# Holding V in the array and streaming the attention weights, in a fused scan, attention and expert kernel

## The chip, the cores and the metric

One Trainium2 chip, one of its cores. The metric is the device time of one execution in microseconds (us); of several executions the median is given. The engines are TensorE (PE in the rows, its weight loads PEld), VectorE (DVE), ScalarE (ACT) and GpSimd (POOL); SP is the queue that issues the transfers.

## The reference

The input is 16 sequences of 256 rows of 128 features, f32. Each is normalised over its features, giving xn. The output is x + scan(xn) + ffn(xn). The scan is a depthwise convolution, a step size from a matmul and a sigmoid, and a state recurrence in 16 states. The other branch is what the change touches:

```
h = layernorm(xn, ln_g, ln_b)
q, k, v = h @ Wq, h @ Wk, h @ Wv            # 16 heads of 64
q, k = l2norm(q) * q_scale, l2norm(k) * k_scale
logits = (q @ k^T) * 10, causal mask
attn = softmax(logits)
out = (attn @ v) joined over heads @ Wo
```

Then come another layernorm, a gate (softmax over 8 experts), all 8 experts (128 to 512, gelu, 512 to 128), their gated sum and a last layernorm.

## The kernel before, in words

The sequences run through a software pipeline. `bodies` calls a prologue, 16 times `body(i, ...)` and a tail, on every engine; each engine runs its own list of work in the order in which it is written, and 60-odd semaphores tie them. Body i does the attention of sequence i, the projections of sequence i+1 (`project`, `project_v`), and the output projection and the experts of sequence i-1. A body has two parts.

The **weighing part** is the loop over k from 0 to 9. The 16 heads are worked as 8 pairs. On TensorE (lines 535 to 556) step k issues, in this order: `scores(i, k)` (L398), which fills S2 with logits of pair k, keys in the partitions; `weigh(i, k-1)` (L415); `project(i+1, k)` (L309 to L311), in the last two steps two `project_v`; for k below 2 half of `output(i-1)` (L431); single turns; and `turn_o(i, k-2)` (L422). ScalarE takes the exponential of the scores (`exps`, L674) into P32, a ring of three buffers; GpSimd sets the triangle above the diagonal to zero (`select`, L830) and squares the projections (`square`, L814). So P32 holds, for each head of a pair, the weights P transposed: keys in the partitions, queries along the columns, 256 columns for the first block of 128 keys and 128 columns for the second, since the other queries come before those keys.

`weigh` works in f32. P is held in the array (128 keys by 128 queries) and V is streamed: Vx has 66 columns per head, 64 of values, and a column of ones at 64, whose product is the softmax's sum. For a pair there are six matmuls (two heads, and three blocks of the causal triangle) into four blocks of 66 columns of O[p % 2], with queries in the partitions. An f32 matmul stands in the trace as two MATMUL records with a weight load each, so 12 for a pair. A `transpose` stands as one. `divide` on VectorE (L1018, L1021) takes the reciprocals of the four sums, 4 numbers in a partition, and multiplies them into the 256 values, giving On. `turn_o` transposes On through the array, two transposes, back into O. `copy_ot` on ScalarE (L680) copies that to OT, 64 features by 2 heads in the partitions, queries along the columns, which `output` of the next body holds as weights. O0 and O1 are two banks of PSUM in turns: `weigh(p)` waits for `ot_done` of pair p-2 (line 409).

VectorE's list of the weighing part (lines 1230 to 1256) begins step k with `divide(i, k-2)`, and then `qk_sums(i+1, k-2)` (L967), the steps of three layernorms (`E_AT`, `O_AT`, `G_AT`), and for seven values of k one state of the scan (`SCAN_AT`; L1113 and L1123).

The **expert part** is the loop over m from 0 to 9: the experts of sequence i-1 (L483 to L485, L701, L499, L1084), the turning of q and k of sequence i+1 (L344), and its score maxima (L358, L362, L1012). The remaining nine states of the scan run there on VectorE. GpSimd scales q and k (`units`, L822) around the border of the parts.

Of the kernel before, what the change touches and what calls it, by code (L numbers as in the profile page):

```python
# [10 lines left out]
ACT = mybir.ActivationFunctionType  # L11
AX = mybir.AxisListType

NSEQ, SEQ, D = 16, 256, 128
P = 128
T = SEQ // P
H, DH = 16, 64
NP = H // 2
HD = H * DH
# [2 lines left out]
DS = 16  # L22
NJ = 4 * T
NL = NP
VW = DH + 2
WS = 64.0
LN_EPS, L2_EPS = 1e-5, 1e-12
QK_SCALE = 10.0
# [12 lines left out]
def build(nc, x, a_log, b, c, dt_w, dt_b, conv_w, conv_b, ln_g, ln_b, Wq, Wk, Wv, q_scale, k_scale,  # L41
          Wo, gate_w, gate_b, w1, b1, w2, b2, out):
    ctx = ExitStack()
    with ctx:
        def sb(name, shape, dt=F32):
            return ctx.enter_context(nc.sbuf_tensor(name, shape, dt))

        def sem(name):
# [3 lines left out]
        ident = sb("ident", [P, P])  # L52
# [62 lines left out]
        QTl = sb("QTl", [P, NP, SEQ], F16)  # L115
        KTh = sb("KTh", [P, NP, SEQ], F16)
        KTl = sb("KTl", [P, NP, SEQ], F16)
        Vx = sb("Vx", [P, T, H, VW])

        mxn = sb("mxn", [P, T, 2, P])  # L120
        mT = sb("mT", [P, 2, SEQ], BF16)
        P32 = sb("P32", [P, 3, 2, 2 * SEQ])
        rr = sb("rr", [P, 2, 2 * T])
        On = sb("On", [P, 2, T, 2 * DH])
        OT = sb("OT", [P, NP, SEQ])

        ost = sb("ost", [P, T, 6])
# [53 lines left out]
        O = [ctx.enter_context(nc.psum_tensor(f"O{n}", [P, 512], F32)) for n in range(2)]  # L181
# [5 lines left out]
            g_vec g_act g_tr  # L187
            qk_ready qk_raw qk_sq qk_sum n_vec n_act unit t_ready t_hi t_lo v_ready v_done
            m_ready mx_done mt_ready mt_done
            st_ready ex_done sel_done pv_done rr_done on_done ot_ready ot_done  # L190
            wo_ready wo_copied o_vec o_act o_tr o_gate o_gT o_b2
            w1_ready gelu_done w2_ready acc_done
            c_vec dt_ready tanh_done a_done scan_done y_done
# [4 lines left out]
         g_vec, g_act, g_tr,  # L198
         qk_ready, qk_raw, qk_sq, qk_sum, n_vec, n_act, unit, t_ready, t_hi, t_lo, v_ready, v_done,
         m_ready, mx_done, mt_ready, mt_done,  # L200
         st_ready, ex_done, sel_done, pv_done, rr_done, on_done, ot_ready, ot_done,
         wo_ready, wo_copied, o_vec, o_act, o_tr, o_gate, o_gT, o_b2,
         w1_ready, gelu_done, w2_ready, acc_done,
         c_vec, dt_ready, tanh_done, a_done, scan_done, y_done,
# [12 lines left out]
        def from_one(eng, semaphore, value):  # L217

            if not isinstance(value, int) or value > 0:
                eng.wait_ge(semaphore, value)  # L220
# [72 lines left out]
        def _(pe):  # L293
# [107 lines left out]

            def weigh(s, p, before):

                pe.wait_ge(sel_done, s * NP + p + 1)
                if p == 0:
                    pe.wait_ge(v_done, (s + 1) * 2 * T)
                if p < 2 and before:
                    pe.wait_ge(acc_done, (s - 1) * NE * T - 2 * (1 - p))
                from_one(pe, ot_done, s * NP + p - 1)
                for t in range(T):  # L410
                    for a in range(2):
                        dst = O[p % 2][:, (2 * t + a) * VW:(2 * t + a + 1) * VW]
                        for kb in range(t + 1):
                            c0 = kb * SEQ + (t - kb) * P
                            last = mm(dst, P32[:, p % 3, a, c0:c0 + P], Vx[:, kb, 2 * p + a, :],  # L415
                                      start=(kb == 0), stop=(kb == t))
                last.then_inc(pv_done, 1)

            def turn_o(s, p):
                pe.wait_ge(on_done, s * NP + p + 1)  # L420
                for t in range(T):
                    last = tr(O[p % 2][:, t * P:(t + 1) * P], On[:, p % 2, t, :], ident[:, :])  # L422
                last.then_inc(ot_ready, 1)

            def output(s, t, before):
                if t == 0:
# [107 lines left out]
            def body(i, older, old, new, newer):  # L534
                for k in range(NP + 2):
                    if k < NP:
                        scores(i, k)
                    if k == 0:
                        turn_max(i, 1)
                    if 1 <= k <= NP:  # L540
                        weigh(i, k - 1, older)
                    if new and k < NP:
                        project(i + 1, k)
                    if new and k >= NP:
                        project_v(i + 1, 2 * (k - NP))
                        project_v(i + 1, 2 * (k - NP) + 1)
                    if old and k < T:
                        output(i - 1, k, older)
                    if old and k == 3:
                        turn_y(i - 1)  # L550
                    if old and k == 6:
                        turn_z2(i - 1)
                    if old and k == 7:
                        gate_logits(i - 1)
                    if k >= 2:
                        turn_o(i, k - 2)
                for m in range(NE + 2):
                    if old and m == 0:
                        expert_up(i - 1, 0)
                    if new and m in TURN_AT:  # L560
                        turn_qk(i + 1, TURN_AT[m])
                        turn_qk(i + 1, TURN_AT[m] + 1)
                    if old and m == 1:
                        turn_gate(i - 1, (i + 1) * NP)
                    if new:
                        for p in MAX_AT.get(m, ()):
                            scores_for_max(i + 1, p)
                    if old and 1 <= m < NE:
                        expert_up(i - 1, m)
                    if old and m == 1:  # L570
                        gated_b2(i - 1)
                    if old and 1 <= m <= NE:
                        expert_down(i - 1, m - 1, (i + 1) * NP)
                    if newer and m == 6:
                        turn(i + 2)
                    if new and m == 7:
                        step_sizes(i + 1)
                    if new and m == 8:
                        turn_max(i + 1, 0)
                    if not old and m == NE + 1:  # L580
                        pe.wait_ge(w1_low, 2)
# [20 lines left out]
        def _(act):  # L602
# [27 lines left out]
            def copy_v(s, j):  # L630
                t, w = divmod(j, 2)
                act.wait_ge(v_ready, s * 2 * T + j + 1)
                if j == 0:
                    from_one(act, pv_done, s * NP)
                fn(Vx[:, t, w * 8:(w + 1) * 8, 0:DH], J[j % 2][:, :].rearrange("p (h d) -> p h d", d=DH),  # L635
                   ACT.Copy, scale=1.0 / WS).then_inc(v_done, 1)

            def high(s, n):
# [32 lines left out]
            def exps(s, p):  # L671
                act.wait_ge(st_ready, s * NP + p + 1)
                from_one(act, pv_done, s * NP + p - 2)
                fn(P32[:, p % 3, :, 0:SEQ + P], S2[:, :, 0:SEQ + P], ACT.Exp).then_inc(ex_done, 1)  # L674

            def copy_ot(s, p):
                act.wait_ge(ot_ready, s * NP + p + 1)
                if p == 0:
                    from_one(act, wo_ready, s)
                fn(OT[:, p, :], O[p % 2][:, 0:SEQ], ACT.Copy).then_inc(ot_done, 1)  # L680

            def decay(s, d):

# [59 lines left out]

            def body(i, older, old, new, newer):
                for k in range(NP + 2):
                    if k >= 3:
                        copy_ot(i, k - 3)
                    if old and k == 2:
                        copy_output(i - 1)
                    if k < NP:  # L750
                        exps(i, k)
                    if k == 0:
                        copy_max(i, 1)
                    if new and 1 <= k <= NP:
                        copy_raw(i + 1, k - 1)
                    if older and k == 0:
                        last_norm(i - 2)
                    if old and k == 4:
                        root_o(i - 1)
                    if newer and k == 5:  # L760
                        norm(i + 2)
                    if new and k == 6:
                        norm_qk(i + 1, 0)
                    if k < NP:
                        decay(i, 2 * k)
                        decay(i, 2 * k + 1)
                    if new and k == 9:
                        copy_v(i + 1, 0)
                        copy_v(i + 1, 1)
                    if old and k == 9:  # L770
                        gate_exps(i - 1)
                if new:
                    copy_v(i + 1, 2)
                copy_ot(i, NP - 1)
                if new:
                    copy_v(i + 1, 3)
                    norm_qk(i + 1, 1)
# [109 lines left out]
        def _(dve):  # L887
# [126 lines left out]

            def divide(s, p):
                dve.wait_ge(pv_done, s * NP + p + 1)
                heads = O[p % 2][:, 0:2 * T * VW].rearrange("p (h d) -> p h d", d=VW)
                V.reciprocal(rr[:, p % 2, :].unsqueeze(2), heads[:, :, DH:DH + 1]).then_inc(rr_done, 1)  # L1018
                dve.wait_ge(rr_done, s * NP + p + 1)
                from_one(dve, ot_ready, s * NP + p - 1)  # L1020
                V.tensor_tensor(On[:, p % 2, :, :].rearrange("p t (a d) -> p (t a) d", d=DH), heads[:, :, 0:DH],  # L1021
                                rr[:, p % 2, :].unsqueeze(2).broadcast_to([P, 2 * T, DH]), ALU.mult
                                ).then_inc(on_done, 1)

            def o_step(s, n):
                at = s * KO
# [129 lines left out]
            def prologue():  # L1156
# [3 lines left out]
                V.memset(xnT[:, :], 0.0)  # L1160
                V.memset(gate[:, :, :].rearrange("p t e -> p (t e)"), 0.0)
                V.memset(mxn[:, :, :, :].rearrange("p t g c -> p (t g c)"), 0.0)
                V.memset(Vx[:, :, :, :].rearrange("p t h d -> p (t h d)"), 1.0)
                dve.wait_ge(const_pool, 7)
                V.tensor_copy(identb[:, :], ident[:, :]).then_inc(const_vec, 1)
                V.tensor_copy(maskb[:, :], mask[:, :]).then_inc(const_vec, 1)
# [165 lines left out]
```

## Time and profile before

| | us |
|---|---|
| median of 3 runs | 1340.16 (1338.81 to 1340.35) |
| the profiled execution | 1340.11 |
| its span, first to last instruction | 1338.4 |
| TensorE busy | 1180.9 (88%) |
| VectorE busy | 1048.9 (78%) |
| ScalarE busy | 752.7 (56%) |
| GpSimd busy | 368.5 (28%) |
| mean granted TensorE clock | 0.915 of full speed |

How to read it: the records of matmuls overlap, and their ends are modelled, so what a matmul costs in a row of them is the distance from one start to the next and not its mean duration. 1.7 us of the profiled execution's own time lie outside its span. The chain is followed back from the last instruction to what released each step.

### The profile page before, as it was taken

The numbers are of one execution on the slowest core, as the hardware profiler recorded it, in microseconds if no ns is written. First come the engines' busy times: TensorE is split into PE (matmuls) and PEld (weight loads), VectorE is DVE, ScalarE is ACT, GpSimd is POOL, SyncE is SP. The second block draws the span as 40 slices with busy tenths as digits, with TensorE's granted clock in tenths as the row PEclk, the third lists the DMA queues.
The fourth block names the chain that finished last, engine by engine and source line by source line (L and its number), as shares of the span: only waits on it lengthen the run. The fifth ranks groups of instructions, "written<-read, shape, count | busy, mean of one in ns | idle before, by whom it ended". The sixth has DMA issues, their size and how long they took to land.

```text
span 1338.4 us, 27838 instructions
## 1 busy us (share of the span) xinstructions
PE 1180.9 (88%) x10435; PEld 954.6 (71%) x10435; DVE 1048.9 (78%) x2718; ACT 752.7 (56%) x1740; POOL 368.5 (28%) x403
## 2 busy tenths in 40 slices
PE   3584989899998989989898998989899898989978
PEld 1363768586786868778685877868587786868877
DVE  7779677888878888887888888788888778787652
ACT  4263655556565565656556465655646565564644
POOL 1151422405133150513315051331505133150100
PEclk9595989899998989989898998989999998999889
DMA  6001000000000000000000000000000000000000
GB/s 177 5 1 40 2 1 13 1 9 5 9 5 2 13 1 10 5 9 6 1 13 1 10 5 9 6 1 10 5 9 6 8 7 5 2 9 2 5 5 5
DMA packets 18724, 14.62 MB, mean 11 GB/s; under 512 B 2408, under 2 KB 16160, under 8 KB 18592
## 3 DMA queue, kind: packets, MB, share of 16 engines
q1 hardware_dynamic: 17680, 12.76, 3.3%
q8 instruction: 84, 1.38, 0.4%
q14 instruction: 48, 0.39, 0.1%
q10 hardware_dynamic: 912, 0.09, 0.0%
HBM read 10.75 MB, written 2.10 MB: 10 GB/s over the span
## 4 chain that ended last, share of the span: by engine, by line
PE 76%; DVE 10%; ACT 9%; issue 3%; POOL 0%; SPq 0%; DMA 0%; DVEq 0%; POOLq 0%; ACTq 0%
PE O L499 17%; PE O L415 11%; PE S L398 7%; PE U L431 4%; PE U L483 4%; PE U L484 4%; PE U L485 4%; PE J L344 4%; PE S L362 3%; PE J L309 3%; PE J L311 3%; PE J L310 3%; PE S L358 3%; PE O L422 2%; ACT hid L701 2%
## 5 line engine op out<-in xcount | busy, mean ns | idle before, releaser
L701 ACT ACTIVATE hid<-U,b1c 128x256 f32<-128x256 f32 x512 | 202.9, 474 | 202.1 <-PE U L485 201.2
L830 POOL TENSOR_SCALAR_AFFINE_SELECT P<-P 128x512 f32<-128x512 f32 x128 | 83.8, 655 | 774.3 <-ACT P L674 774.3
L499 PE MATMUL O<-w2s,hid 128*128 128x128 f32 x2048 | 251.5, 276 | 0.0
L499 PEld LDWEIGHTS O<-w2s,hid 128*128 128x128 f32 x2048 | 238.5, 192 | 2.9
L415 PE MATMUL O<-Vx,P 128*128 128x66 f32 x1536 | 200.8, 281 | 9.1 <-ACT OT L680 9.0
L1113 DVE TENSOR_TENSOR_SCAN st<-aexp,u 128x256 f32<-128x256 f32 x256 | 196.9, 769 | 4.7 <-ACT aexp L686 4.7
L415 PEld LDWEIGHTS O<-Vx,P 128*128 128x128 f32 x1536 | 183.0, 193 | 24.1 <-issue 12.5
L822 POOL TENSOR_TENSOR raw<-raw,nr 128x512 f32<-128x512 f32 x128 | 140.2, 1119 | 115.9 <-DVE nr L986 88.8
L483 PE MATMUL U<-h2h,w1h 128*128 128x256 f16 x512 | 149.3, 292 | 0.0
L484 PE MATMUL U<-h2l,w1h 128*128 128x256 f16 x512 | 148.8, 291 | 0.0
L485 PE MATMUL U<-h2h,w1l 128*128 128x256 f16 x512 | 148.0, 289 | 0.0
L1084 DVE SCALAR_TENSOR_TENSOR acc<-O,gate,acc 128x128 f32<-128x128 f32 x256 | 78.0, 346 | 87.2 <-PE O L499 85.3
L344 PE MATMUL J<-ident,raw 128*128 128x128 f32 x512 | 80.3, 305 | 66.5 <-DVE QTl L997 58.9
L674 ACT ACTIVATE P<-S 128x768 f32<-128x768 f32 x128 | 103.8, 811 | 56.8 <-PE S L398 56.6
L1123 DVE SCALAR_TENSOR_TENSOR y<-st,bc,y 128x256 f32<-128x256 f32 x240 | 129.5, 540 | 8.0
L1012 DVE TENSOR_REDUCE mxn<-S 128x2 f32<-128x256 f32 (+1 forms) x256 | 130.1, 551 | 5.9 <-PE S L362 5.6
L814 POOL TENSOR_TENSOR sq<-raw 128x512 f32<-128x512 f32 x120 | 130.5, 1087 | 0.0
L344 PEld LDWEIGHTS J<-ident,raw 128*128 128x128 f32 x512 | 66.1, 158 | 72.7 <-POOL raw L822 67.1
L686 ACT ACTIVATE aexp<-dt,negA 128x256 f32<-128x256 f32 x256 | 115.0, 500 | 0.0
L967 DVE TENSOR_REDUCE ssq<-sq 128x8 f32<-128x512 f32 x128 | 87.2, 681 | 28.9 <-POOL sq L814 28.6
L680 ACT ACTIVATE OT<-O 128x256 f32<-128x256 f32 x128 | 48.8, 381 | 105.8 <-PE O L422 105.7
L309 PE MATMUL J<-wh,hTh 128*128 128x512 f16 x192 | 82.4, 429 | 15.2 <-ACT Vx L635 14.5
(163 smaller groups left out, 2148.6 us busy)
## 6 DMA issues: line engine op xcount, KB each, us to landing
xin<-in_L_attn_x SPq DMA_DIRECT2D x16, 128.0 KB, 2.2
xres<-in_L_attn_x SPq DMA_DIRECT2D x16, 128.0 KB, 2.4
hid<-in_L_ffn_w SPq DMA_DIRECT2D x2, 1024.0 KB, 6.2
out_dram<-fin SPq DMA_DIRECT2D x16, 128.0 KB, 1.8
raw<-in_L_ffn_Wq SPq DMA_DIRECT2D x1, 512.0 KB, 4.3
raw<-in_L_ffn_Wk SPq DMA_DIRECT2D x1, 512.0 KB, 6.6
raw<-in_L_ffn_Wv SPq DMA_DIRECT2D x1, 512.0 KB, 7.5
wos<-in_L_ffn_Wo SPq DMA_DIRECT2D x1, 512.0 KB, 11.0
```

Source lines behind the costliest of these rows:

```text
L344: last = tr(J[n % 2][:, (a * T + t) * P:(a * T + t + 1) * P], raw[:, chunk(t, kind, half), c0:c0 + P], ident[:, :])
L415: last = mm(dst, P32[:, p % 3, a, c0:c0 + P], Vx[:, kb, 2 * p + a, :], start=(kb == 0), stop=(kb == t))
L483: mm(dst, w1h[:, f:f + P], h2h[:, :], start=True, stop=False)
L484: mm(dst, w1h[:, f:f + P], h2l[:, :], start=False, stop=False)
L485: last = mm(dst, w1l[:, f:f + P], h2h[:, :], start=False, stop=True)
L499: last = mm(O[e % 2][:, t * P:(t + 1) * P], hid[:, e % 2, m, t * P:(t + 1) * P], w2s[:, e * FC + m, :], start=(m == 0), stop=(m == FC - 1))
L701: fn(hid[:, e % 2, f % FC, :], U[q % 2][:, m * SEQ:(m + 1) * SEQ], ACT.Gelu_apprx_tanh, bias=b1c[:, f:f + 1], scale=1.0 / WS).then_inc(gel ...
L814: nc.gpsimd.tensor_tensor(sq[:, j % 2, :], raw[:, j, :], raw[:, j, :], ALU.mult).then_inc(qk_sq, 1)
L822: nc.gpsimd.tensor_tensor(group, group, nr[:, j * 8:(j + 1) * 8].unsqueeze(2).broadcast_to([P, 8, DH]), ALU.mult).then_inc(unit, 1)
L1012: V.tensor_reduce(mxn[:, t, g, hh:hh + DH + 2:DH + 1], S2[:, :, t * P:(2 * t + 1) * P], AX.X, ALU.max, negate=True).then_inc(mx_done, 1)
L1113: V.tensor_tensor_scan(st[:, d % 2, :], aexp[:, d, :], u[:, :], 0.0, ALU.mult, ALU.add).then_inc(scan_done, 1)
L1123: V.scalar_tensor_tensor(y[:, s % 2, :], st[:, d % 2, :], bc[:, d:d + 1], y[:, s % 2, :], ALU.mult, ALU.add).then_inc(y_done, 1)
```

## The change

- `weigh` holds V in the array instead of P. A head's V block is 128 keys by 64 values, so it fills half of the array's columns; head 0 of the pair takes columns and output partitions 0 to 63, head 1 takes 64 to 127. P is streamed, 256 columns for the first block of keys and 128 for the second. Columns 0 to 255 of O then hold the weighed values already as features by queries.
- The same four matmuls run a second time with a held 128 by 64 matrix of ones. Columns 256 to 511 of O hold each head's sum, repeated in its 64 partitions.
- `divide` takes the reciprocal of all those 256 columns, and one multiply writes OT.
- `turn_o`, `copy_ot`, On and the ones in Vx are gone. Vx is dense. `ones` is a new tile.

```diff
-        Vx = sb("Vx", [P, T, H, VW])
+        Vx = sb("Vx", [P, T, HD])
+        ones = sb("ones", [P, DH])
-        rr = sb("rr", [P, 2, 2 * T])
-        On = sb("On", [P, 2, T, 2 * DH])
+        rr = sb("rr", [P, 2, SEQ])
...
                 from_one(pe, ot_done, s * NP + p - 1)
-                for t in range(T):
-                    for a in range(2):
-                        dst = O[p % 2][:, (2 * t + a) * VW:(2 * t + a + 1) * VW]
-                        for kb in range(t + 1):
-                            c0 = kb * SEQ + (t - kb) * P
-                            last = mm(dst, P32[:, p % 3, a, c0:c0 + P], Vx[:, kb, 2 * p + a, :],
-                                      start=(kb == 0), stop=(kb == t))
+                for n in range(2):
+                    for kb in range(T):
+                        for a in range(2):
+                            c0 = n * SEQ
+                            values = Vx[:, kb, (2 * p + a) * DH:(2 * p + a + 1) * DH]
+                            last = mm(O[p % 2][a * DH:(a + 1) * DH, c0 + kb * P:c0 + SEQ],
+                                      (values, ones[:, :])[n],
+                                      P32[:, p % 3, a, kb * SEQ:kb * SEQ + SEQ - kb * P],
+                                      start=(kb == 0), stop=(kb == T - 1), skip_group_check=True)
                 last.then_inc(pv_done, 1)
...
             def divide(s, p):
                 dve.wait_ge(pv_done, s * NP + p + 1)
-                heads = O[p % 2][:, 0:2 * T * VW].rearrange("p (h d) -> p h d", d=VW)
-                V.reciprocal(rr[:, p % 2, :].unsqueeze(2), heads[:, :, DH:DH + 1]).then_inc(rr_done, 1)
+                V.reciprocal(rr[:, p % 2, :], O[p % 2][:, SEQ:2 * SEQ]).then_inc(rr_done, 1)
                 dve.wait_ge(rr_done, s * NP + p + 1)
-                from_one(dve, ot_ready, s * NP + p - 1)
-                V.tensor_tensor(On[:, p % 2, :, :].rearrange("p t (a d) -> p (t a) d", d=DH), heads[:, :, 0:DH],
-                                rr[:, p % 2, :].unsqueeze(2).broadcast_to([P, 2 * T, DH]), ALU.mult
-                                ).then_inc(on_done, 1)
+                if p == 0:
+                    from_one(dve, wo_ready, s)
+                V.tensor_tensor(OT[:, p, :], O[p % 2][:, 0:SEQ], rr[:, p % 2, :], ALU.mult).then_inc(ot_done, 1)
```

Besides, `turn_o` and its call are taken from TensorE's list, `copy_ot` and its two calls from ScalarE's, and `copy_v` writes 512 dense columns. Nothing else moves.

## Rows read from the trace of the kernel before

**Rows 1.** The page's chain that ended last, shares of the span.

```profile
PE 76%; DVE 10%; ACT 9%; issue 3%; POOL 0%; SPq 0%; DMA 0%; DVEq 0%; POOLq 0%; ACTq 0%
```

**Rows 2.** Busy time by stretch in one middle body: weighing part (two rows), expert part.

```profile
core 0: us, PE busy (x) PEld busy (x) DVE busy (x) ACT busy (x) POOL busy (x), PEclk, DMA share, GB/s
530.40:552.40 22.00, 21.85 (x235) 18.17 (x236) 15.47 (x54) 16.47 (x38) 9.01 (x11) 1.00 0.03 7
552.40:568.20 15.80, 13.89 (x98) 9.58 (x99) 14.81 (x35) 9.43 (x25) 9.15 (x9) 0.89 0.01 2
568.20:609.10 40.90, 36.48 (x322) 31.48 (x321) 34.07 (x83) 20.29 (x49) 5.29 (x5) 0.92 0.03 8
```

**Rows 3.** Timeline of TensorE, step 3 of that body: start us, us.

```profile
541.92 0.28 PE L398 MATMUL S<-mT,sel 64*128 64x256 bf16 x2
...
542.68 1.55 PE L415 MATMUL O<-Vx,P 128*128 128x66 f32 x12
544.07 0.38 PE L309 MATMUL J<-wh,hTh 128*128 128x512 f16 x1
544.29 0.38 PE L310 MATMUL J<-wh,hTl 128*128 128x512 f16 x1
```

**Rows 4.** Timeline of VectorE, the first `divide` of that body.

```profile
536.48 0.18 DVE L1018 RECIPROCAL rr<-O 128x4 f32<-128x4 f32 x1 [1.64 <-PE O L415]
```

**Rows 5.** The same timeline, the last `divide` of that body.

```profile
565.74 0.18 DVE L1018 RECIPROCAL rr<-O 128x4 f32<-128x4 f32 x1
```

**Rows 6.** VectorE's waits in the weighing part (530 to 571): total us, times, longest.

```profile
DVE rr L1018 <- PE O L415: 3.1, 4, 1.6
DVE ssq L967 <- POOL sq L814: 1.9, 4, 0.6
...
DVE nu L979 <- ACT ny L615: 0.4, 1, 0.4
```

**Rows 7.** Groups by line: count, busy us, mean ns, idle before and releaser.

```profile
L1018 DVE RECIPROCAL rr<-O 128x4 f32<-128x4 f32 x128 | 22.9, 179 | 55.9 <-PE O L415 55.9
L1063 DVE RECIPROCAL grs<-gs 128x2 f32<-128x2 f32 x16 | 2.5, 159 | 0.6 <-ACT ge L669 0.6
L1183 DVE COPY wcol<-J 128x8 f32<-128x8 f32 x1 | 0.2, 157 | 0.0
L1184 DVE COPY b1c<-J 128x32 f32<-128x32 f32 x1 | 0.2, 181 | 0.0
L1074 DVE COPY acc<-O 128x256 f32<-128x256 f32 x16 | 6.8, 425 | 15.1 <-PE O L468 15.1
L1021 DVE TENSOR_TENSOR On<-O,rr 128x256 f32<-128x256 f32 x128 | 54.3, 425 | 4.4
```

**Rows 8.** The two reciprocal lines: ns min/median/max.

```profile
L1018 DVE RECIPROCAL rr<-O x128: 168/182/183, 71.3 to 1261.5; 128x4 f32<-128x4 f32 x128
L1063 DVE RECIPROCAL grs<-gs x16: 157/158/166, 173.4 to 1302.3; 128x2 f32<-128x2 f32 x16
```

**Rows 9.** The chain in order of time: start us, us, what.

```profile
541.77 0.22 PE O L422 x2
...
558.77 0.28 PE O L422 x2
...
559.08 0.39 ACT OT L680
559.47 0.14 issue
```

**Rows 10.** The same view: an f32 matmul of 256 columns, and a projection matmul at the lower clock.

```profile
526.89 0.43 PE J L506 x2
...
561.22 0.43 PE J L309
```

**Rows 11.** Busy time in the divide stretches of the first and the last body.

```profile
71.30:97.50 26.20, 23.85 (x228) 17.68 (x225) 19.68 (x41) 18.50 (x41) 16.86 (x19) 1.00 0.01 2
1241.40:1261.60 20.20, 19.62 (x219) 17.43 (x218) 15.24 (x48) 12.79 (x28) 5.07 (x8) 0.98 0.03 8
```

More of the change, by code:

```diff
@@ L24 @@
 NL = NP
-VW = DH + 2
 WS = 64.0
@@ L189, in build @@
             m_ready mx_done mt_ready mt_done
-            st_ready ex_done sel_done pv_done rr_done on_done ot_ready ot_done
+            st_ready ex_done sel_done pv_done rr_done ot_done
             wo_ready wo_copied o_vec o_act o_tr o_gate o_gT o_b2
@@ L200, in build @@
          m_ready, mx_done, mt_ready, mt_done,
-         st_ready, ex_done, sel_done, pv_done, rr_done, on_done, ot_ready, ot_done,
+         st_ready, ex_done, sel_done, pv_done, rr_done, ot_done,
          wo_ready, wo_copied, o_vec, o_act, o_tr, o_gate, o_gT, o_b2,
@@ L409, in weigh @@
                 from_one(pe, ot_done, s * NP + p - 1)
-                for t in range(T):
-                    for a in range(2):
-                        dst = O[p % 2][:, (2 * t + a) * VW:(2 * t + a + 1) * VW]
-                        for kb in range(t + 1):
-                            c0 = kb * SEQ + (t - kb) * P
-                            last = mm(dst, P32[:, p % 3, a, c0:c0 + P], Vx[:, kb, 2 * p + a, :],
-                                      start=(kb == 0), stop=(kb == t))
-                last.then_inc(pv_done, 1)
[L419 to L423, printed above, removed]
+                for n in range(2):
[7 more added lines that the diff above has]
+                                      start=(kb == 0), stop=(kb == T - 1), skip_group_check=True)
+                last.then_inc(pv_done, 1)
             def output(s, t, before):
@@ L554, in body @@
                         gate_logits(i - 1)
-                    if k >= 2:
-                        turn_o(i, k - 2)
                 for m in range(NE + 2):
@@ L634, in copy_v @@
                     from_one(act, pv_done, s * NP)
-                fn(Vx[:, t, w * 8:(w + 1) * 8, 0:DH], J[j % 2][:, :].rearrange("p (h d) -> p h d", d=DH),
+                fn(Vx[:, t, w * 512:(w + 1) * 512], J[j % 2][:, :],
                    ACT.Copy, scale=1.0 / WS).then_inc(v_done, 1)
@@ L674, in exps @@
                 fn(P32[:, p % 3, :, 0:SEQ + P], S2[:, :, 0:SEQ + P], ACT.Exp).then_inc(ex_done, 1)
[L676 to L680, printed above, removed]
             def decay(s, d):
@@ L745, in body @@
                 for k in range(NP + 2):
-                    if k >= 3:
-                        copy_ot(i, k - 3)
                     if old and k == 2:
@@ L773, in body @@
                     copy_v(i + 1, 2)
-                copy_ot(i, NP - 1)
                 if new:
@@ L1162, in prologue @@
                 V.memset(mxn[:, :, :, :].rearrange("p t g c -> p (t g c)"), 0.0)
-                V.memset(Vx[:, :, :, :].rearrange("p t h d -> p (t h d)"), 1.0)
+                V.memset(ones[:, :], 1.0)
                 dve.wait_ge(const_pool, 7)
```

## The prediction, made before the change was run

> **What bounds the kernel now.** I read four views. The chain that ended last says where the span is spent: three quarters of it on TensorE, a tenth on VectorE [rows 1]. That is a mean over two different parts, so the busy time by stretch comes next [rows 2]. In the first 22 us of a weighing part TensorE is never idle. In its last 16 us VectorE is the full engine (14.8 of 15.8 us), TensorE waits, and its clock falls. In the expert part TensorE leads again, with VectorE 34 of 41 us busy. The third view, VectorE's waits, says how much room it has in the weighing part: 0.82 us or so before the second `divide`, 0.4 before most `qk_sums` [rows 6]. So there are two resources here with little slack, TensorE and VectorE, and the change moves work from ScalarE and TensorE to VectorE. The fourth view, the groups by line, prices it. The profiled execution took 1340.11 us, the median of three is 1340.16, so I work against 1340.1.
>
> **TensorE, per pair.** Before: the 12 f32 records of `weigh` start at 542.68 and the next matmul at 544.07, so 1.39 us [rows 3], 0.115 each, for 66 streamed columns. An f32 record of 256 columns takes 0.43/2 = 0.215 us [rows 10], so 66 columns would need 0.055. What sets 0.115 is therefore the load of 128 f32 weight columns. After: eight matmuls, 16 records, of 256 and 128 columns, that is 8 of 0.215 and 8 of 0.108, 2.58 us if they run one behind the other; the loads of 64 columns, half as many as before, hide. If the two heads' halves ran wholly side by side it would be 1.29. The 16 matmuls of a step's scores show halves of the rows side by side [rows 3]: one behind the other, 8 of 256 and 8 of 128 f16 columns would take 8 × 0.108 + 8 × 0.054 = 1.30 us, and from 541.92 to 542.68 they take 0.76. Halves of the columns are shown nowhere. I take side by side, but in the order of issue: both records of head 0, then both of head 1. The second record of one head can then overlap the first of the other, but the first and last of the list stand alone; followed through with 0.215 and 0.108 that gives 1.60 us. So `weigh` costs +0.2 us, with bounds −0.1 and +1.2. The removed `turn_o` gives back 0.22 [rows 9]. Sum about 0.
>
> The Trainium skill (TensorEngine Tiling (Array Packing), When to Use Tiling) speaks for the change: with 64 or fewer columns to stream, swap the operands and use two column tiles, for up to twice the speed. By it the pair would take 1.29 us; the row on the halves of the rows agrees as far as it goes.
>
> **ScalarE, per pair.** One copy goes. In the chain of `divide`, turn, copy and the next `weigh` that shows where TensorE waits, 0.28 + 0.39 + 0.14 = 0.8 us go [rows 9], once or twice in a body. It is worth something only while that chain sets the pace.
>
> **VectorE, per pair.** The multiply stays: 128x256, 0.425 us [rows 7]. The reciprocal grows from 128x4 to 128x256, and this is the term that decides. A copy of 256 columns out of the same PSUM tile takes 0.425 us, so a reciprocal at one element per step would cost +0.24 us. But the two reciprocal lines don't read like copies. A PSUM copy of 8 elements takes 157 ns and one of 32 takes 181: 1.0 ns per element over 149 fixed [rows 7]. The reciprocal of 4 elements takes 182 [rows 8], as long as the copy of 32. (182 − 149)/4 = 8.3 ns per element, eight steps of an element. The one of 2 elements takes 158: (158 − 142 to 149)/2 is 5 to 8. The wide stride of its operand is no excuse, since the multiply reads the same strided tile at 0.425 for 256, as a copy does. So I take 149 + 256 × 8.3 = 2.28 us, +2.1 us per pair. Bounds: the least times of the two lines, 168 and 157, give 5.5 ns per element, 1.56 us (+1.4); their medians 182 and 158 give 12, 3.2 us (+3.0); and, if the 24 ns come from elsewhere, +0.24.
>
> The Trainium skill (VectorE: DVE Perf Modes, First, the fixed hardware budget) says that the reciprocal is an iterated division with a repeat count of 8. By that rule the time per element is eight steps, and the row at 182 ns agrees.
>
> **The sum.** `divide` is the head of VectorE's step k, and everything behind it in that list waits: `qk_sums`, the layernorm steps, the scan. In a middle body first and last `divide` start 29.3 us apart [rows 4, 5] (the 14 middle bodies are alike). Eight reciprocals add 8 × 2.1 = 16.8 us. Inside the stretch VectorE idles 1.5 us for `weigh` (3.1 less the 1.6 before the first), 1.9 for GpSimd's squares and 0.4 for ScalarE, 3.8 in all [rows 4, 6]; the longer `divide` covers these. That leaves +13.0 us. VectorE's seven steps then take 40.2 us, 5.7 each, against TensorE's 0.76 + 1.6 + 0.65 + gaps = 3.3 at full clock, so VectorE sets the pace from step 2 on, and the two zero sums above (turn, copy) are worth nothing. The expert part, which starts from units and turned q and k that hang on VectorE's last steps, moves back whole. In the first body the idle share is 26.2 − 19.7 = 6.5, in the last 20.2 − 15.2 = 5.0 [rows 11]: +10.3 and +11.8. In all 14 × 13.0 + 22 = 204 us.
>
> Then the clock. Where TensorE waited in steps 7 to 9 it went to 1.2 GHz, a projection matmul took 0.43 us [rows 10] instead of 0.22 [rows 3], and the stretch's mean clock was 0.89 [rows 2]. Now it waits some 2.4 us in every step. At the lower level its step takes 2 × 3.0 + 0.3 = 6.3 us, 0.6 more than VectorE's; being busy then, it should rise again. Bounds 0 and 8 × 0.6 = 4.8 us a body; I take 0.7, 10 us in all. 1340.1 + 204 + 10 = **1554 us**. With 1.4 and 3.0 us for the reciprocal in place of 2.1 it would be about 1465 and 1660.
>
> **The rivals.**
> - Cheap reciprocal, halves side by side; faster. VectorE gains 0.24 × 8 = 1.9 us a body, half of it covered by its idle time, TensorE between 0 and −0.33 a pair in the five steps where it leads (+0 to −1.6), and the removed turn and copy give 0.8 to 1.2. Between +0.2 and −1.8 us a body: 1311 to 1343, middle 1325. It decides if the reciprocal of 256 elements takes under 0.8 us. For it: nothing here shows a wide reciprocal, and 33 ns are a small lever to multiply by 64. The swap rule of the Trainium skill named above would hold in this case only.
> - Cheap reciprocal, halves one behind the other. +1.2 − 0.2 = +1.0 us a pair, full in five steps and half in three, 6.5 a body: 1444.
> - Dear reciprocal and dear array. TensorE's step is 4.3 us at full clock, still under 5.7, but 8.3 at the lower level. With half of the steps there, 4 × 2.6 = 10.4 us in each of 14 bodies in place of 0.7: about 1690; with a quarter, 1617. I put 1640.
> - The change doesn't do what it says: no VectorE or TensorE instruction would then differ, but the shapes of both are in the diff; its chance is under 0.01 and stands in none of the sums.
>
> **How the numbers follow.** Dear reciprocal, as forecast: 0.78. Dear in both: 0.08. Cheap, side by side: 0.09. Cheap, in line: 0.05. The likeliest case's own range is 1480 to 1610. To leave out no more than 2 in 10 the range reaches up to the third rival and down over part of the lower bound of the reciprocal: 1470 to 1645. Runs of this kernel differ by 0.1%, so about 0.2% can be told from no change. Slower by over 0.2%: 0.78 + 0.08 + 0.05 + 0.01 of the first rival = 0.92. Within: 0.02. Faster: 0.06.
>
> **What would show it.** Right: the reciprocal's group near 2.28 us × 128 (292 us), VectorE near 85% busy ((1049 + 269)/1554) and first in the chain, step distances of `divide` near 5.7 us, ScalarE's L680 gone, and the expert part's length unchanged. TensorE: 16 records of L415's successor within 1.6 to 1.7 us at full clock. Wrong: a reciprocal under 1 us refutes the forecast. Records at 2.6 us per pair refute side by side. A weighing part with VectorE idle while TensorE is full at 1.2 GHz means that the array is the new bound.

## The result, and the profile after

The changed kernel takes 1481.03 us, median of 4 runs (1477.8 to 1482.34), against 1339.49 us before (4 runs). The ratio is 1.1062, 95% interval 1.1041 to 1.1082: 10.6% slower. The profiled execution took 1482.34 us. The forecast was 1554 us, slower, in a range from 1470 to 1645: the direction and the mechanism came out, the size was too large by half (+214 forecast, +142 measured). The result lies 11 us above the lower end of the range.

The page of the changed kernel, busy time and then shares of the chain that ended last, by engine:

```profile
PE 1184.2 (80%) x10691; PEld 896.8 (61%) x10691; DVE 1254.5 (85%) x2718; ACT 715.1 (48%) x1612; POOL 387.1 (26%) x403
...
PE 48%; DVE 31%; issue 14%; POOL 5%; ACT 1%; SPq 0%; DMA 0%; DVEq 0%; POOLq 0%; ACTq 0%
```

VectorE's share of the chain went from 10% to 31% [rows 1], but TensorE's is still the larger; how far this view can be trusted is said with the experiments. VectorE has as many instructions as before, 2718, and is busy 205.6 us longer. Its groups by line (count, busy us, mean ns, idle before):

```profile
L1002 DVE RECIPROCAL rr<-O 128x256 f32<-128x256 f32 x128 | 223.5, 1746 | 27.2 <-PE O L415 27.2
L1006 DVE TENSOR_TENSOR OT<-O,rr 128x256 f32<-128x256 f32 x128 | 54.4, 425 | 15.9 <-PE U L427 12.0
L1096 DVE TENSOR_TENSOR_SCAN st<-aexp,u 128x256 f32<-128x256 f32 x256 | 199.3, 779 | 4.9 <-ACT aexp L674 4.7
L1106 DVE SCALAR_TENSOR_TENSOR y<-st,bc,y 128x256 f32<-128x256 f32 x240 | 146.2, 609 | 8.0
```

The reciprocal went from 22.9 to 223.5 us [rows 7]: 200.6 of the 205.6. The multiply costs what it did. The wait before `qk_sums` is gone, covered as foreseen [rows 6]. A new wait of 12.0 us stands before the multiply, for the output projection (L427).

Busy time between the first and the last `divide` of a middle body, in the kernel before and then in the changed one (columns as in [rows 2]):

```profile
536.50:565.80 29.30, 27.39 (x248) 20.72 (x247) 24.52 (x64) 18.80 (x47) 16.90 (x19) 0.94 0.02 6
```

```profile
758.40:796.20 37.80, 29.86 (x280) 18.99 (x279) 35.97 (x63) 18.03 (x42) 18.00 (x19) 0.91 0.02 5
```

VectorE was idle for 4.8 of 29.3 us, and is now idle for 1.8 of 37.8. TensorE was idle for 1.9 us and is now idle for 7.9. The stretch is 8.5 us longer. The middle bodies follow each other every 87.9 us, where it was 78.7 (mean distance of their first divides), so 8.5 of the 9.2 us lie between the divides. The rest of a body holds the eighth reciprocal and grew by 0.8 us, so the expert part is no longer than it was.

The timeline of TensorE, in step 3 and then in step 6:

```profile
764.56 0.87 PE L415 MATMUL O<-P,Vx 128*64 128x256 f32 x8
765.26 0.82 PE L415 MATMUL O<-P,ones 128*64 128x256 f32 x8
766.01 0.39 PE L308 MATMUL J<-wh,hTh 128*128 128x512 f16 x1
...
775.28 0.87 PE L415 MATMUL O<-P,Vx 128*64 128x256 f32 x8 [1.12 <-DVE OT L1006]
```

The halves of the columns do run side by side: the 16 records take 1.45 us from the first start to the next matmul, 8 in 0.70 us for the values and 8 in 0.75 for the sums, where one behind the other they would need 2.58. The scores of a step take 0.76 of 1.30 us [rows 3], about the same share. The last row shows `weigh` itself waiting 1.12 us for VectorE's multiply.

### The profile page after: what moved, and what is told of

It reads as the page before. It is cut to its first block, busy times and chain, and to the rows that moved or that the text cites. A ratio compares the mean times of both kernels' runs of the same rounds, so it can differ in the third digit from the quotient of the medians.

```text
span 1480.6 us, 28096 instructions
## 1 busy us (share of the span) xinstructions
PE 1184.2 (80%) x10691; PEld 896.8 (61%) x10691; DVE 1254.5 (85%) x2718; ACT 715.1 (48%) x1612; POOL 387.1 (26%) x403
## 4 chain that ended last, share of the span: by engine, by line
PE 48%; DVE 31%; issue 14%; POOL 5%; ACT 1%; SPq 0%; DMA 0%; DVEq 0%; POOLq 0%; ACTq 0%
PE O L495 16%; DVE rr L1002 10%; POOL raw L807 4%; DVE ssq L952 4%; PE U L427 4%; PE U L479 4%; PE U L480 4%; PE J L343 4%; PE U L481 4%; DVE y L1106 3%; DVE st L1096 3%; PE S L361 3%; PE S L357 3%; PE S L397 2%; PE O L415 2%
## 5 line engine op out<-in xcount | busy, mean ns | idle before, releaser
L815 POOL TENSOR_SCALAR_AFFINE_SELECT P<-P 128x512 f32<-128x512 f32 x128 | 90.7, 709 | 770.4 <-ACT P L668 770.4
L1002 DVE RECIPROCAL rr<-O 128x256 f32<-128x256 f32 x128 | 223.5, 1746 | 27.2 <-PE O L415 27.2
L807 POOL TENSOR_TENSOR raw<-raw,nr 128x512 f32<-128x512 f32 x128 | 148.9, 1188 | 204.6 <-DVE nr L971 177.5
L343 PE MATMUL J<-ident,raw 128*128 128x128 f32 x512 | 86.0, 323 | 115.3 <-POOL raw L807 111.9
L1106 DVE SCALAR_TENSOR_TENSOR y<-st,bc,y 128x256 f32<-128x256 f32 x240 | 146.2, 609 | 8.0
L415 PE MATMUL O<-P,Vx 128*64 128x256 f32 (+1 forms) x1024 | 121.5, 361 | 38.4 <-DVE OT L1006 38.3
L343 PEld LDWEIGHTS J<-ident,raw 128*128 128x128 f32 x512 | 71.7, 168 | 121.3 <-POOL raw L807 115.9
L799 POOL TENSOR_TENSOR sq<-raw 128x512 f32<-128x512 f32 x120 | 132.8, 1107 | 30.0 <-DVE ssq L952 29.3
L415 PE MATMUL O<-P,ones 128*64 128x256 f32 (+1 forms) x1024 | 117.1, 351 | 0.0
L415 PEld LDWEIGHTS O<-P,Vx 128*64 128x64 f32 x1024 | 70.3, 145 | 72.0 <-issue 50.7
L629 ACT ACTIVATE Vx<-J 128x512 f32<-128x512 f32 x64 | 36.4, 590 | 139.4 <-PE J L310 139.1
```

The source lines that it names most:

```text
L343: last = tr(J[n % 2][:, (a * T + t) * P:(a * T + t + 1) * P], raw[:, chunk(t, kind, half), c0:c0 + P], ident[:, :])
L415: last = mm(O[p % 2][a * DH:(a + 1) * DH, c0 + kb * P:c0 + SEQ], (values, ones[:, :])[n], P32[:, p % 3, a, kb * SEQ:kb * SEQ + SEQ - kb * ...
L799: nc.gpsimd.tensor_tensor(sq[:, j % 2, :], raw[:, j, :], raw[:, j, :], ALU.mult).then_inc(qk_sq, 1)
L807: nc.gpsimd.tensor_tensor(group, group, nr[:, j * 8:(j + 1) * 8].unsqueeze(2).broadcast_to([P, 8, DH]), ALU.mult).then_inc(unit, 1)
L1002: V.reciprocal(rr[:, p % 2, :], O[p % 2][:, SEQ:2 * SEQ]).then_inc(rr_done, 1)
L1106: V.scalar_tensor_tensor(y[:, s % 2, :], st[:, d % 2, :], bc[:, d:d + 1], y[:, s % 2, :], ALU.mult, ALU.add).then_inc(y_done, 1)
```

## The experiments

All times are medians beside runs of the kernel before on the same chip. Three chips were used, and on them the kernel before gave 1338.1, 1338.6 and 1337.0 us. Eleven more kernels ran.

**The width of the reciprocal alone, taken out.** Of the division only 4 columns are computed, the rest of rr is 1.0.

```diff
-                V.reciprocal(rr[:, p % 2, :], O[p % 2][:, SEQ:2 * SEQ]).then_inc(rr_done, 1)
+                V.reciprocal(rr[:, p % 2, 0:4], O[p % 2][:, SEQ:SEQ + 4]).then_inc(rr_done, 1)
...
```

> Changed kernel with a reciprocal of 4 columns (128x4) in place of 256; the rest of rr holds 1.0, so nearly all of the division is left out. Everything else of the change stays. Theory (the wide reciprocal on VectorE is the whole loss): the reciprocal goes back to about 0.18 us, the loss of 141 us goes, and since the array's part is about even (1.45 us against 1.39 + 0.22) and a copy on ScalarE is gone, 1310 to 1340 us. Rival (the doubled streaming or the chain through TensorE costs as well): 1370 us or more.

Measured: 1331.99 us, ratio 0.9956 (0.994 to 0.9972). The whole loss goes with the width, and 6 us more. The new layout by itself is no loss. More than half of the gain lies in the first and the last body: the middle ones follow each other every 78.4 us, against 78.7 in the kernel before. VectorE waits 35.7 us for the output projection here.

**The width alone, put into the kernel before.**

```diff
-                V.reciprocal(rr[:, p % 2, :].unsqueeze(2), heads[:, :, DH:DH + 1]).then_inc(rr_done, 1)
+                V.reciprocal(rr[:, p % 2, :, :], heads[:, :, 2:DH + 2]).then_inc(rr_done, 1)
...
```

> Kernel before, with the reciprocal taken of 64 columns of each head block (128x256 in all, the sums among them) in place of the 4 sums; the multiply reads the same 4 results. Output as before. Theory: +1.57 us in each of the 128 divides, 3.8 us of a middle body's idle time covered: 8.8 us a body, plus the chain of turn and copy that here still hangs behind it, 1475 to 1500 us. Rival (the cost comes with the new layout, not with the width): under 1400 us.

Measured: 1421.03 us, ratio 1.0623 (1.0605 to 1.0642). Neither the 1475 to 1500 us of the theory nor the rival's "under 1400" came, and so this is a miss: the same 1747 ns reciprocal costs 83 us here and 149 in the new layout (1481 − 1332). Its page says where the difference is:

```profile
PE 1197.5 (84%) x10435; PEld 969.8 (68%) x10435; DVE 1198.6 (84%) x2718; ACT 753.1 (53%) x1740; POOL 362.3 (26%) x403
```

VectorE has the same list of work and the same reciprocal, and yet is busy 56 us less than in the changed kernel; the spans differ by 60. Two of its groups make 34 of the 56 us, here in this kernel, against 779 and 609 ns in the changed one:

```profile
L1113 DVE TENSOR_TENSOR_SCAN st<-aexp,u 128x256 f32<-128x256 f32 x256 | 186.9, 730 | 4.7 <-ACT aexp L686 4.7
L1123 DVE SCALAR_TENSOR_TENSOR y<-st,bc,y 128x256 f32<-128x256 f32 x240 | 124.6, 519 | 8.0
```

Most of the rest is in smaller groups: `nw` takes 216 ns in the mean against 594 in the changed kernel, `h2l` 426 against 1056, `ove` 159 against 648.

The changed kernel's timeline shows what happens to such an instruction:

```profile
788.00 2.27 POOL L807 TENSOR_TENSOR raw<-raw,nr 128x512 f32<-128x512 f32 x2
788.23 1.15 DVE L1030 TENSOR_TENSOR h2l<-h2T,h2h 128x256 f16<-128x256 f32 x1
...
789.30 1.52 DVE L1096 TENSOR_TENSOR_SCAN st<-aexp,u 128x256 f32<-128x256 f32 x1
790.86 0.48 DVE L1106 SCALAR_TENSOR_TENSOR y<-st,bc,y 128x256 f32<-128x256 f32 x1
```

Beside GpSimd's two products the scan takes 1.52 us. Its median is 0.684, and the `y` step, which starts after them, is at its undisturbed 0.48. In the kernel before with the wide reciprocal the same place of a body looks like this:

```profile
756.54 2.04 POOL L822 TENSOR_TENSOR raw<-raw,nr 128x512 f32<-128x512 f32 x2
...
758.76 0.42 DVE L1047 TENSOR_TENSOR h2l<-h2T,h2h 128x256 f16<-128x256 f32 x1
759.11 0.68 DVE L1113 TENSOR_TENSOR_SCAN st<-aexp,u 128x256 f32<-128x256 f32 x1
```

The products end at 758.58, before `h2l` starts, and both operations take their short time. So VectorE's work has a size that depends on what GpSimd does at that moment.

**Pieces of the reciprocal.** In 1, 2, 4 or 8 pieces by the pair's number modulo 4.

```diff
+                parts = (1, 2, 4, 8)[p % 4]
+                w = SEQ // parts
+                for n in range(parts):
+                    last = V.reciprocal(rr[:, p % 2, n * w:(n + 1) * w], O[p % 2][:, SEQ + n * w:SEQ + (n + 1) * w])
...
```

> Changed kernel; the reciprocal of 256 columns is taken in 1, 2, 4 or 8 pieces, by the pair's number modulo 4. Tells the fixed part from the part per element. If it is 6.24 ns per element over 149 ns (from 1746 ns at 256): pieces of 128, 64 and 32 columns take 948, 548 and 349 ns. If it is 8.3 ns per element at few columns and something else at many: 32 columns would take about 415 ns. In time, in each 4 pairs 0 + 1 + 3 + 7 = 11 more fixed parts of 0.06 to 0.15 us, 22 a body: +20 to +50 us on 1481.

One run, 1487.06 us: +6, less than expected. Groups by shape:

```profile
L1005 DVE RECIPROCAL rr<-O 128x32 f32<-128x32 f32 x256 | 58.5, 299 | 0.0
L1005 DVE RECIPROCAL rr<-O 128x64 f32<-128x64 f32 x128 | 56.7, 506 | 0.0
L1005 DVE RECIPROCAL rr<-O 128x128 f32<-128x128 f32 x64 | 56.2, 917 | 0.0
L1005 DVE RECIPROCAL rr<-O 128x256 f32<-128x256 f32 x32 | 56.1, 1754 | 26.5 <-PE O L415 26.5
```

(1754 − 299)/224 = 6.5 ns per element at every width (6.5, 6.4, 6.5 between neighbours), where a copy takes 1.0 [rows 7]. The pieces of 128, 64 and 32 columns were expected at 948, 548 and 349 ns, so the part per element was put too low and the fixed part too high. The records of neighbouring pieces overlap: eight of them are busy 58.5/32 = 1.83 us a pair, and not 8 × 0.299. Against one whole reciprocal, 56.1/32 = 1.75, a further piece costs about 0.01 us, which is why the time rose so little.

**The two heads one after the other.** The same matmuls, in another order:

```diff
-                for n in range(2):
-                    for kb in range(T):
-                        for a in range(2):
+                for a in range(2):
+                    for n in range(2):
+                        for kb in range(T):
```

> Changed kernel with the two heads' matmuls one head after the other (all 8 records of head 0, then all 8 of head 1), so that the halves of the columns hardly overlap; the work is the same. weigh should take about 2.6 us in place of 1.45. Theory (VectorE sets the pace of the weighing part, 4.3 to 7 us a step): most of 1.15 us a pair is covered, 1481 to 1510 us. Rival (TensorE's chain of scores, weigh, divide sets it): 8 x 1.15 = 9.2 us a body, about 1620 us.

Measured: 1461.82 us, ratio 1.0926 (1.0906 to 1.0946), 19 us *faster* than the changed kernel, with TensorE busy 46 us longer. Neither theory had that, and `weigh` was expected at 2.6 us. The timeline shows that the edit did its work, 2.15 us for a pair in place of 1.45, with only the middle records side by side:

```profile
600.84 0.86 PE L415 MATMUL O<-P,Vx 128*64 128x256 f32 x4
601.54 0.38 PE L415 MATMUL O<-P,ones 128*64 128x256 f32 x1
601.54 0.43 PE L415 MATMUL O<-P,Vx 128*64 128x256 f32 x1
...
602.25 0.81 PE L415 MATMUL O<-P,ones 128*64 128x256 f32 x4
602.99 0.39 PE L308 MATMUL J<-wh,hTh 128*128 128x512 f16 x1
```

VectorE was busy 1230.1 us, 24.4 less than in the changed kernel, with the same list: 12.1 of them in `nw`, 7.9 in `ove`, 7.9 in `y`. That is the gain. The traces show how it comes about for `nw`, first in the changed kernel and then here:

```profile
781.11 1.04 POOL L799 TENSOR_TENSOR sq<-raw 128x512 f32<-128x512 f32 x1
781.14 1.06 DVE L968 TENSOR_TENSOR nw<-nu,ny 128x32 f32<-128x32 f32 x1
```

```profile
773.18 0.19 DVE L968 TENSOR_TENSOR nw<-nu,ny 128x32 f32<-128x32 f32 x1
```

In the changed kernel `nw` starts with one of GpSimd's squares and lasts as long as it. Here GpSimd is idle from 771.83 to 774.04 us, and `nw` takes 0.19. A later `weigh` shifts GpSimd's operations against VectorE's.

There is a rival to this: TensorE's mean granted clock is 0.926 here and 0.887 in the changed kernel. It is not the cause. The gain lies between the first and the last `divide` of a middle body, 36.0 us in place of 37.8, and VectorE is busy for 34.2 us there in place of 36.0. The rest of the body, where TensorE leads, takes 50.5 us in place of 50.1.

The page of this run also warns of one view. The chain that ended last gives VectorE 7% here, GpSimd 21% and "issue" 30%, with VectorE as full as in the changed kernel, where it had 31%. The chain's shares by engine do not tell which engine sets the pace in these kernels; the busy time of the stretch and the experiments do.

**The same order with the narrow reciprocal.** Both edits above; the division is left out here too.

> Both edits: heads one after the other on TensorE, and the narrow reciprocal of 4 columns (the rest of rr is 1.0, the division left out). With the division cheap, TensorE has no cover in the weighing part. If side by side matters there: 8 x (2.0 - 1.45) = 4.4 us a body or more over the narrow one, 1332 + 70 = about 1400 us. Rival (GpSimd's squares and selects set the step, as the chain of the narrow version hints with 21% on GpSimd, and TensorE has slack again): 1330 to 1350 us.

Measured: 1386.39 us, ratio 1.0367 (1.034 to 1.0395), 54 us more than the narrow one, and near the 1400 of the first theory. With the division cheap TensorE has no cover, and the halves side by side are worth that.

**GpSimd's part cut, in both kernels.** The scaling of q and k covers 128x8 in place of 128x512, so their normalisation is left out, and a factor 1/512 stands in their copies.

```diff
-                    group, group, nr[:, j * 8:(j + 1) * 8].unsqueeze(2).broadcast_to([P, 8, DH]),
+                    group[:, :, 0:1], group[:, :, 0:1], nr[:, j * 8:(j + 1) * 8].unsqueeze(2),
...
```

> Changed kernel; GpSimd's units scale one of 64 columns of each head (128x8 in place of 128x512), so the normalisation of q and k is left out; the copies of q and k carry a factor 1/512 to keep the numbers in range. VectorE's list is the same. Theory (GpSimd's long operations stretch VectorE's beside them: scan 683 to 1524 ns, y 485 to 1081 ns): these forms fall back to 0.68 and 0.49 us, VectorE's busy time falls by 40 us or more, and the time by 40 to 90 us, some of it because units no longer hold up TensorE. Rival (the stretching has another cause, such as PSUM reads of TensorE's neighbours): VectorE's busy time stays within 10 us of 1254.

Measured on the changed kernel: 1439.55 us, 41 less than 1481.03, at the lower end of what was expected, and VectorE's busy time 1254.5 → 1204.4. The scan's mean is 706 ns and `y` 537. They did not fall all the way. GpSimd's squares and selects are still there, and that these make the rest is not tested.

> Kernel before, with GpSimd's units cut to one of 64 columns as in the run on the changed kernel (normalisation of q and k left out). There it gave 41 us and took 50 us off VectorE's busy time. Theory (the stretching costs most where VectorE has no idle time): in the kernel before VectorE loses 25 to 40 us of busy time and the time falls by less than on the changed kernel, 10 to 30 us. Rival (units cost as a link of the chain, not by stretching): the same 41 us or more.

Measured on the kernel before: 1328.04 us, ratio 0.9928 (0.99 to 0.9956), 9 us less, with VectorE 1048.9 → 996.4. The busy time falls by 52 us, more than the 25 to 40 expected and as much as in the changed kernel, and buys a fifth of the time; the 9 us lie just under the 10 to 30 expected. The direction of both halves of the theory holds: GpSimd stretches VectorE in either kernel, and it costs where VectorE is the bound. The traces sharpen it. In the kernel before, the first `divide` starts at 63.4 us in place of 71.3, and a middle body takes 78.5 us in place of 78.7: most of the gain lies ahead of the first body's divides, before the pipeline runs, where the rival (a link of the chain) fits better. In the changed kernel 4.6 us lie there, and each middle body is 2.6 us shorter (85.3 in place of 87.9).

**OT doubled**, so that the multiply of pair 0 needs not wait for the output projection.

```diff
-                    from_one(dve, wo_ready, s)
+                    from_one(dve, wo_ready, s - 1)
-                V.tensor_tensor(OT[:, p, :], O[p % 2][:, 0:SEQ], rr[:, p % 2, :], ALU.mult).then_inc(ot_done, 1)
+                V.tensor_tensor(OT[:, s % 2, p, :], O[p % 2][:, 0:SEQ], rr[:, p % 2, :], ALU.mult).then_inc(ot_done, 1)
```

> Changed kernel with OT doubled, by sequence, so that the multiply of pair 0 no longer waits for the output projection of the sequence before (a wait that stood on ScalarE's copy before, and that the change put on VectorE: 12 us of VectorE's idle time). If VectorE sets the pace, those 12 us come off: 1468 to 1475 us. Rival (it only moves into the next wait): 1478 to 1482 us.

Measured: 1467.56 us, ratio 1.0973 (1.0947 to 1.0998), 13.5 less than the changed kernel. The moved wait was a loss of its own.

**The reciprocal on ScalarE.** The kernel's own list loads the table of Ln and Exp for the weighing part, so the change adds no table load (37 before and after it), and ScalarE was busy for only half of the time.

```diff
+            def roots(s, p):
+                act.wait_ge(pv_done, s * NP + p + 1)
+                from_one(act, ot_done, s * NP + p - 1)
+                fn(rl[:, p % 2, :], O[p % 2][:, SEQ:2 * SEQ], ACT.Ln).then_inc(rl_done, 1)
+                act.wait_ge(rl_done, s * NP + p + 1)
+                fn(rr[:, p % 2, :], rl[:, p % 2, :], ACT.Exp, scale=-1.0).then_inc(rr_done, 1)
...
```

> Changed kernel with the reciprocal moved to ScalarE, which holds the table of Ln and Exp through the weighing part: Ln of the sums, 128x256, then Exp of minus that, at the head of its step k, ahead of the exponentials of pair k. VectorE keeps the multiply alone. Theory (the division on VectorE is the loss, and the new layout is worth a little): like the kernel with the narrow reciprocal, 1315 to 1340 us, ScalarE +115 us busy. Rival (ScalarE's step becomes the chain, since Ln and Exp stand ahead of the exponentials that TensorE waits for): 1360 us or more.

Measured: 1312.73 us, ratio 0.9814 (0.9793 to 0.9835), 2 us under the range expected. ScalarE is busy 794.9 us, 80 more than in the changed kernel and not 115.

> The same with the multiply behind qk_sums in VectorE's step, so that VectorE does not stand idle for Ln and Exp (about 1 us after weigh). Theory: 0 to 10 us less than the version with the multiply first. Rival (qk_sums waits for GpSimd's square and now delays OT and with it weigh): up to 20 us more.

Measured: 1309.01 us, ratio 0.9783 (0.9761 to 0.9805). The late multiply is worth 3.7 us, within what was expected. This version beats both kernels: 2.2% under the kernel before, 172 us under the changed one. From its page and its groups:

```profile
PE 1135.4 (87%) x10691; PEld 866.6 (66%) x10691; DVE 1025.9 (78%) x2590; ACT 794.7 (61%) x1868; POOL 385.5 (29%) x403
...
PE 63%; DVE 18%; ACT 14%; issue 5%; DMA 1%; SPq 0%; DVEq 0%; ACTq 0%
```

```profile
L676 ACT ACTIVATE rr<-rl 128x256 f32<-128x256 f32 x128 | 53.3, 417 | 4.0
L674 ACT ACTIVATE rl<-O 128x256 f32<-128x256 f32 x128 | 47.8, 374 | 18.5 <-PE O L416 18.5
```

Ln and Exp take 0.79 us together where VectorE's reciprocal took 1.75, on an engine with room. The middle bodies take 76.7 us each, where they took 78.7 in the kernel before.

> Reciprocal on ScalarE by Ln and Exp, multiply behind qk_sums, and OT doubled. There VectorE waited 14.4 us for the output projection. If that counts: 1297 to 1304 us; if TensorE leads there (63% of its chain), 1307 to 1310 us as without it.

Measured: 1311.39 us, ratio 0.9805 (0.978 to 0.9829), no gain over 1309.01, and about what was expected if TensorE leads. The wait that cost 13.5 us with VectorE as the bound costs nothing here.

## Why the prediction was right, and where it was off

**VectorE sets the pace: right.** A table of its busy and idle time (span less busy), from the pages, makes the sum:

| kernel | span | VectorE busy | idle |
|---|---|---|---|
| before | 1338.4 | 1048.9 | 289.5 |
| changed | 1480.6 | 1254.5 | 226.1 |
| width in the kernel before | 1420.2 | 1198.6 | 221.6 |
| heads one after the other | 1458.6 | 1230.1 | 228.5 |
| units cut, changed | 1437.1 | 1204.4 | 232.7 |
| OT doubled, changed | 1464.9 | 1252.5 | 212.4 |
| pieces | 1485.3 | 1258.6 | 226.7 |
| narrow | 1329.7 | 1072.0 | 257.7 |
| in line and narrow | 1383.4 | 1062.3 | 321.1 |

In the six kernels with the wide reciprocal the idle time stays within 212 to 233 us and the span follows the busy time. In the three with a narrow one it does not. The signs named beforehand came as follows: VectorE 85% busy, as foreseen; L680 gone; the steps of `divide` 37.8/7 = 5.4 us apart where 5.7 was foreseen; the expert part no longer than before. "First in the chain" did not come, TensorE has 48% and VectorE 31%.

**The reciprocal, +2.1 us: the mis-sized term.** Slower than a copy by the element was right, 8.3 ns for it was not. It is (1746 − 149)/256 = 6.2 ns, 1.75 us in all, +1.57 a pair. The forecast read 33 ns of a 4-element instruction; its lower bound, 5.5 ns and 1465 us, was nearer to the result than the value taken. The value itself lay 73 us too high, and the range held because it reached down toward that lower bound. With 1.57 the forecast's own sum is 8 × 1.57 − 3.8 = 8.8 us in 14 bodies, (12.6 − 6.5) and (12.6 − 5.0) in the first and last: 1340.1 + 137 = 1477, without the clock term. By the Trainium skill (VectorE: DVE Perf Modes, First, the fixed hardware budget) the division has a repeat count of 8; the estimate of eight steps per element gives 2.28 us, and the measured 1.75 us decides. Two slips of the working changed nothing: 3.0 us for the reciprocal gives 1669 by the same sum with its clock term, not 1660, and the lower value from the 2-element line is (158 − 149)/2 = 4.5 ns, not 5; no row shows the 142.

**Idle time covered, 3.8 us a middle body: right in size, in part by luck.** All idle time fell by 63.4 us over 16 bodies, against 14 × 3.8 + 6.5 + 5.0 = 65. But the new wait adds 12 us to it, so about 75 us of the old idle time were covered, and two errors of 10 to 12 us cancel.

**Terms left out.** The change moved the wait for the output projection from ScalarE to VectorE; the prediction listed the moved parts and did not price it. It is 12 us of idle time, and the run without it is 13.5 us faster. The stretching by GpSimd was in the kernel before too, but the prediction took VectorE's other work as fixed. In this change it came to no more than 205.6 − 200.6 = 5 us of busy time, which is luck, since the same list varied by 56 us between kernels.

**The clock, 10 us: not seen.** TensorE's clock did fall further (0.887 mean against 0.915). In the body shown TensorE waits 4.6 us for VectorE's `h2T`, up to 787.4, and the next `weigh` takes 2.8 us at 1.2 GHz (788.3 to 791.1, granted clock 0.50). But VectorE is busy for 2.76 of these 2.80 us. Between the divides it has 1.8 us of idle time in 37.8, 0.8 of them for the output projection, so the slow `weigh` did not hold it up.

**TensorE, 1.60 us a pair, sum about 0: 1.45.** The halves of the columns overlap almost whole (1.45 where wholly side by side would be 1.29), so the hand-followed order of issue was too pessimistic. In this point the Trainium skill (TensorEngine Tiling (Array Packing), When to Use Tiling) was nearer: by its factor of two the pair is estimated at 1.29 us, and the trace shows 1.45 to the next matmul's start. "Worth nothing" was right for the pair (1.39 + 0.22 before, 1.45 after) as long as VectorE leads.

**The rivals.** The cheap reciprocal with the halves side by side would have been 1325 us by the prediction. The narrow run stands for it at 1332, and the Ln and Exp runs at 1309. Cheap and in line was put at 1444 and came to 1386, at an order that still overlapped a sixth of the records' time. The dear array did not appear.

Open: how much of the 56 us between the two layouts each shifted operation makes. The traces show `h2l`, the scan and `nw` beside GpSimd's operations in the changed kernel and clear of them in the old layout. That moving these alone would give the time back was not tried.

## What to carry to other kernels

A layout that drops a transpose by replicating a sum over partitions pays for every replica on the engine that inverts it. Before moving an elementwise step to an engine, price it at its new width on that engine, and look for a free engine that has the function's table: here the same layout was 10.6% slower with the reciprocal on VectorE and 2.2% faster with Ln and Exp on ScalarE. When an engine becomes the bound, waits on it and disturbances of it that cost little before are charged in full: cutting GpSimd's part was worth 9 us before and 41 us after, and in a middle body 0.2 and 2.6 us.

## What the runs showed of the hardware beyond what was expected

- A reciprocal on VectorE takes 6.2 to 6.5 ns per element from 32 to 256 columns, six times a copy's. Out of PSUM it took 1723 to 1758 ns in all 128 places of the changed kernel, also where GpSimd worked beside it.
- Two f32 matmuls in halves of the columns run about as fully side by side as f16 ones in halves of the rows: 16 records in 1.45 us of 2.58 in a row, and the scores in 0.76 of 1.30.
- GpSimd's products beside it take a scan on VectorE from 0.68 to 1.52 us, and one of its squares takes `nw`, 32 columns, from 0.19 to 1.06 us. More busy time for TensorE made the kernel 19 us faster by shifting that overlap.
